# Attention on one core: the copy of the turned maxima and the scaling of x move from VectorE to ScalarE

## The chip, the cores and the metric

The kernel runs on one core of one Trainium2 chip. The metric is the device time of one execution in microseconds (us). The time before is the median of 3 runs. One further execution was taken with the profiler on; every row below comes from it.

## The reference, cut to what matters

The program computes two transformer blocks; the change touches only the first attention. There x has 16 sequences of 512 tokens with 128 channels:

```
x = x + attn(layernorm(x))          # layernorm: (x - mean) / sqrt(var + 1e-5), per token
q, k, v = split(layernorm(x) @ W_attn.T)    # 16 heads of 8 channels
scores  = q @ k.T / sqrt(8) + alibi bias, causal
y       = softmax(scores) @ v
```

The layernorm can be written in two ways that give the same numbers up to rounding: (x - mean) * rstd, or x * rstd + shift with shift = -mean * rstd.

## The kernel before, in words

`attention` handles the 16 sequences ("blocks" b = 0 to 15), each in 4 steps (st = 0 to 3) of 4 heads. Every engine runs its own hand-written list of steps (`steps`), and semaphores couple them. Three streams are skewed against each other:

- **Scores for the maximum.** TensorE makes 12 score units per step (S0 to S5, two units each, lines 364 and 368) into three PSUM buffers `psS`, used in turn. VectorE reduces each unit to its row maxima (`mx`, line 472). Unit n can start only when the reduction of unit n-3 is done.
- **Turning of the maxima.** After a step's 12 reductions VectorE splits the maxima into two bf16 parts (`mhl`, lines 481 and 483). In the next step TensorE turns them ("M", line 404) into the PSUM bank `psM`; an engine copies the 8x512 result to `mT` (line 464), and SyncE's queue places it as two rows of the query operand, where it is needed one step later.
- **Scores again, exponential, and values.** TensorE makes the scores once more, with the maximum subtracted (E0 to E5, line 383, three PSUM buffers `psE`), ScalarE takes the exponential of 12 units (line 532, k = 0 to 11), GpSimd clears the future entries (`clear_future`, line 281, one for each of four column groups j), and TensorE multiplies with the values (V0 to V3, line 395). V1 needs the exponentials 4 to 7 and the clearing j = 1 behind them. E5's two units need the exponentials 7 and 8.

TensorE's order in each step is written out in line 139: S0 E0 M V2 S1 E1 V3 S2 E2 S3 E3 V0 S4 E4 S5 E5 V1. V2 and V3 belong to the step before.

The input of a later block is prepared in between. In step 3 of block b VectorE computes mean and variance of block b+2 (`norm_stats`, lines 411 to 421), GpSimd raises the variance to the power -1/2 (`factors`, line 266), and VectorE writes the scaled x into `xn` (`norm_apply`, line 427) in front of its reduction 6. In step 0 of the next block TensorE turns `xn` (line 318) and projects it to q and k (line 324); ScalarE, VectorE (`split`, line 440) and GpSimd (lines 271 and 273) cut these into three bf16 parts, which go through memory into the operands. Blocks 0 and 1 are prepared before the steps begin. So there are 14 preparations inside the steps.

`psM` is one bank that is used in turn, eight times a block; `s_mr` counts its fillings and `s_mf` its releases.

Of the kernel before, what the change touches and what calls it, by code (L numbers as in the profile page):

```python
# [66 lines left out]
def attention(nc, x_all, ident, x_in, w_attnT, qkv_scr, y_scr, rec_scr, shared, c_ident, c_identb, c_maskq, c_rows, nb=NB):  # L67


    with ExitStack() as ctx:  # L70
# [15 lines left out]
        sync6 = sb("sync6", [P, 6], F32)  # L86
        mv = sb("mv", [P, TT, 2], F32)
        veps = sb("veps", [P, TT], F32)
        rstd = sb("rstd", [P, TT], F32)
        mhalf = sb("mhalf", [P, TT], F32)  # L90
        zeros = sb("zeros", [P, T], F32)
        warm = sb("warm", [P, 1], F32)
# [65 lines left out]
        def there(u):  # L158

            return not isinstance(u, int) or 0 <= u < G * nb  # L160
# [61 lines left out]
        def _(pool):  # L222
# [39 lines left out]

            def factors(b):
                pool.wait_ge(s_xn, b)
                pool.wait_ge(s_stat, 3 * b + 3)
                pool.tensor_tensor(rstd[:], veps[:], mhalf[:], ALU.pow).then_inc(s_rstd, 1)

            def split_rest(b, s):

# [139 lines left out]
        @block.vector  # L409
        def _(dve):  # L410
            def norm_stats(b):
                for t in range(TT):
                    bn = dve.bn_stats(stats[:, t], x_all[:, bass.ds(TT * b + t, 1), :].rearrange("p a c -> p (a c)"))
                bn.then_inc(s_stat, 1)
                dve.wait_ge(s_stat, 3 * b + 1)
                dve.tensor_copy(sync6[:], stats[:, TT - 1])
                for t in range(TT):
                    bn = dve.bn_aggr(mv[:, t], stats[:, t])
                bn.then_inc(s_stat, 1)
                dve.wait_ge(s_stat, 3 * b + 2)  # L420
                dve.tensor_scalar(veps[:], mv[:, :, 1], EPS, None, ALU.add).then_inc(s_stat, 1)

            def norm_apply(b, used):
                dve.wait_ge(s_rstd, b + 1)
                dve.wait_ge(s_mr, used)
                for t in range(TT):
                    i = dve.tensor_scalar(xn[:, t], x_all[:, bass.ds(TT * b + t, 1), :].rearrange("p a c -> p (a c)"),
                                          mv[:, t, 0:1], rstd[:, t:t + 1], ALU.subtract, ALU.mult)
                i.then_inc(s_xn, 1)

            dve.wait_ge(s_first, 80)
            norm_stats(0)
            norm_apply(0, 0)
            dve.memset(sync6[:], 0.0).then_inc(s_su, 1)
            dve.tensor_scalar(wT[:, 0], wT[:, 0], D ** -0.5, None, ALU.mult).then_inc(s_yc, 1)

            def split(b, s):
                dve.wait_ge(s_hi, 2 * b + s + 1)
                dve.wait_ge(s_lo, 2 * b + s)
                dve.tensor_tensor(rest[:], psM[:], parts[s][:, 0], ALU.subtract).then_inc(s_mf, 1)  # L440

            for s in range(2):
                split(0, s)
            norm_stats(1)
            norm_apply(1, 1)

            def step(n, b, st, last):
                g = st
                real = there(G * b)
                ahead = st == G - 1 and (not isinstance(b, int) or b + 2 < nb)  # L450
                if ahead:
                    dve.wait_ge(s_rest, REST)
                    norm_stats(b + 2)
                if st == 1 and not last:
                    split(b + 1, 1)
                if real and there(G * b + g - 1):
                    dve.wait_ge(s_hl, 2 * (G * b + g))
                for k in range(UN):
                    if k == 2:
                        if there(G * b + st - 1):  # L460
                            dve.wait_ge(s_mr, use_max(b, st, last) + 1)
                            if there(G * b + st - 2):
                                dve.wait_ge(s_mrow, 32 * (G * b + st - 1))
                            dve.tensor_copy(mT[:], psMb[0:2 * HG, 0:T]).then_inc(s_mf, 1)
                    if k == 6 and ahead:
                        norm_apply(b + 2, use_next(b, 0) + 1)
                    if real:
                        j, p, h0, nh = s_units[k]
                        u = UN * g + k
                        w = P * (j + 1)  # L470
                        dve.wait_ge(s_sr, UN * G * b + u + 1)
                        dve.tensor_reduce(mx[:, j, 2 * p + h0:2 * p + h0 + nh], psS[k % 3][:, 0:nh * w].rearrange("p (h k) -> p h k", h=nh),  # L472
                                          AX, ALU.max).then_inc(s_su, 1)
                    if k == 7 and st == 0 and not last:
                        split(b + 1, 0)
                if real:
                    dve.wait_ge(s_su, 1 + UN * G * b + UN * (g + 1))
                    if there(G * b + st - 1):
                        dve.wait_ge(s_mr, use_max(b, st, last) + 1)
                    by_half = mx[:].rearrange("p t (c h) -> p t c h", c=2)  # L480
                    dve.tensor_copy(mhl[:, :, :, 0], by_half).then_inc(s_hl, 1)
                    dve.wait_ge(s_hl, 2 * (G * b + g) + 1)
                    dve.tensor_tensor(mhl[:, :, :, 1], by_half, mhl[:, :, :, 0], ALU.subtract).then_inc(s_hl, 1)
            steps(dve, step, 1)
            dve.wait_ge(s_sum, 16)
            dve.reciprocal(sums[0][:], sums[0][:]).then_inc(s_inv, 1)

        @block.scalar
        def _(act):
# [9 lines left out]
            def copy_v(n, use):  # L499
                act.wait_ge(s_mr, use + 1)  # L500
                act.activation(vaug[n][:, :, :, 0:D], psM[:].rearrange("p (t h d) -> p t h d", t=TT, h=H), ACT.Copy)\
                   .then_inc(s_mf, 1)

            copy_x(0)
            for s in range(2):
                hi_part(0, s, s + 1)
            act.wait_ge(s_vinit, 3)
            copy_v(0, 3)
            act.activation(warm[:], ident[:, 0:1], ACT.Exp).then_inc(s_ex, 1)

            def copy_y(u, g):
# [5 lines left out]
            def step(n, b, st, last):  # L517
# [10 lines left out]
                for k in range(EN):  # L528
                    if there(u):
                        j, p, h0, nh = e_units[k]  # L530
                        act.wait_ge(s_er, EN * u + k + 1)
                        act.activation(probs[st % 2][j][:, 2 * p + h0:2 * p + h0 + nh, :].rearrange("p h q -> p (h q)"),  # L532
                                       psE[k % 3][:, 0:nh * W[j]], ACT.Exp).then_inc(s_ex, 1)
                        if k == 3 and there(u - 1):
                            copy_y(u - 1, st + 1)
                    if k == 5 and ahead:
                        hi_part(b + 1, 0, use_next(b, 1))
                    if k == 9 and ahead:
                        hi_part(b + 1, 1, use_next(b, 2))
                    if k == 7 and st == 2 and not last:  # L540
                        if isinstance(b, int) and b == 0:
                            act.wait_ge(s_vinit, 4)
                        copy_v(1 - n, use_next(b, 3))
# [1606 lines left out]
```

## Time and profile before

| | us |
|---|---|
| median of 3 runs | 1781.46 (1780.94 to 1782.33) |
| the profiled execution | 1782.71 |
| span of its instructions | 1781.0 |
| attention, from the start of the span to about | 745 |

Busy over the whole span, from the page: TensorE 1289.9 us (72%), VectorE 1214.9 us (68%), GpSimd 1030.5 us (58%), ScalarE 825.2 us (46%). In a row of the timeline stand the start in us, the time that the row covers, the engine, the line, the operation with its tiles, the number of instructions (x4), and in brackets how long the engine had been idle and what ended it. Starts that lie closer together than the durations mean that consecutive instructions overlap.

### The profile page before, as it was taken

To read this page: it belongs to the slowest core of one execution; us is meant where nothing else is said; L and a number is where in the kernel's file an instruction comes from. 1 tells how busy PE (TensorE), PEld (TensorE's weight loads), DVE (VectorE), ACT (ScalarE), POOL (GpSimd) and SP (SyncE) were. 2 spreads that over 40 slices of the span, in tenths; PEclk is the share of its full clock that TensorE was granted. 3 is DMA by queue.
4 is the path that set the end of the run, shared out by engine and by line. 5 is a ranking of instruction groups with operands and counts; after the bars stand their busy time and mean duration, and the time that the engine had idled before them with its cause. 6 is when DMAs were issued, how large, how long until landed. Compare 5 with 4: busy or idle time off the path is not lost. (4 is left out here: it accounts for less than half of the span.)

```text
span 1781.0 us, 34332 instructions
## 1 busy us (share of the span) xinstructions
PE 1289.9 (72%) x8762; PEld 705.7 (40%) x8763; DVE 1214.9 (68%) x3716; ACT 825.2 (46%) x2009; POOL 1030.5 (58%) x1071
## 2 busy tenths in 40 slices
PE   2888888888888888559116266626279999999996
PEld 1333333333333333158006233316246556555654
DVE  2777777777777778457662279877766666666663
ACT  0356666555555656501202166643334444444443
POOL 4455555554555554234005368968158888888886
PEclk9999999998999999855557665555579999999999
DMA  4433322322332333145004300300413333333332
GB/s 99 138 79 79 85 78 77 81 83 69 77 86 77 77 84 81 55 169 200 5 9 113 79 30 24 126 6 24 171 30 42 42 42 42 41 41 43 41 42 35
DMA packets 79454, 124.66 MB, mean 70 GB/s; under 512 B 22976, under 2 KB 47232, under 8 KB 75312
## 3 DMA queue, kind: packets, MB, share of 16 engines
q0 software_dynamic: 45568, 59.38, 18.4%
q1 hardware_dynamic: 25792, 51.63, 8.6%
q10 hardware_dynamic: 8032, 12.93, 2.0%
q8 instruction: 26, 0.43, 0.1%
q14 instruction: 36, 0.29, 0.1%
HBM read 65.65 MB, written 57.68 MB: 69 GB/s over the span
## 5 line engine op out<-in xcount | busy, mean ns | idle before, releaser
L472 DVE TENSOR_REDUCE mx<-psS 128x1 f32<-128x384 f32 (+3 forms) x768 | 426.2, 597 | 164.4 <-PE psS L368 155.0
L532 ACT ACTIVATE probs<-psE 128x512 f32<-128x512 f32 (+2 forms) x768 | 362.5, 529 | 236.7 <-PE psE L383 227.1
L281 POOL TENSOR_SCALAR_AFFINE_SELECT probs<-probs 128x512 f32<-128x512 f32 x256 | 162.3, 641 | 236.4 <-ACT probs L532 236.1
L1935 POOL DMA_INDIRECT out<-ex_y,ex_idx x144 | 236.5, 1643 | 47.9 <-issue 43.0
L395 PE MATMUL psY<-probs,vaug 128*32 128x512 f32 (+3 forms) x2048 | 209.3, 473 | 42.7 <-POOL probs L281 42.6
L364 PE MATMUL psS<-maskq,identb 128*128 128x128 bf16 (+1 forms) x768 | 161.6, 254 | 54.5 <-DVE mx L472 49.9
L1926 POOL DMA_INDIRECT ex_xg<-expert_tab,ex_idx x144 | 142.2, 988 | 66.0 <-issue 41.8
L364 PEld LDWEIGHTS psS<-maskq,identb 128*128 128x128 bf16 x768 | 64.0, 98 | 245.4 <-DVE mx L472 186.7
L1909 DVE SCALAR_TENSOR_TENSOR ex_h<-ex_psG,ex_w,ex_up 128x352 f32<-128x352 f32 x144 | 84.0, 584 | 111.3 <-ACT ex_w L2010 107.1
L383 PE MATMUL psE<-qop,kop 63*128 63x512 bf16 (+3 forms) x1024 | 141.7, 309 | 2.7 <-ACT probs L532 2.7
L368 PE MATMUL psS<-kop,qop 61*128 61x128 bf16 (+3 forms) x1024 | 142.3, 317 | 0.0
L1993 PE MATMUL ex_psY<-ah_w3s,ex_hT 128*128 (+1 forms) x864 | 133.3, 290 | 1.2 <-ACT ex_hT L2004 0.7
L2003 ACT ACTIVATE ex_hT<-ex_psH 128x256 f32<-128x256 f32 x144 | 55.4, 385 | 135.9 <-PE ex_psH L1969 135.9
L1993 PEld LDWEIGHTS ex_psY<-ah_w3s,ex_hT 128*128 128x128 f32 (+1 forms) x864 | 107.5, 191 | 21.9 <-issue 4.3
L1975 PE MATMUL ex_psU<-ah_w1s,ex_xT 128*128 x288 | 110.4, 465 | 0.5 <-ACT ex_xT L2014 0.5
L1976 PE MATMUL ex_psG<-ah_w2s,ex_xT 128*128 x288 | 109.9, 463 | 0.0
L2014 ACT ACTIVATE ex_xT<-ex_psX 128x128 f32<-128x128 f32 x144 | 40.0, 278 | 104.9 <-PE ex_psX L1962 104.7
L395 PEld LDWEIGHTS psY<-probs,vaug 128*32 128x32 f32 x2048 | 46.8, 112 | 88.1 <-POOL probs L281 46.7
L1962 PE MATMUL ex_psX<-ident,ex_xg 128*128 128x128 f32 x144 | 47.5, 330 | 39.1 <-DMA ex_xg<-expert_tab,ex_idx 38.5
L271 POOL TENSOR_TENSOR parts<-rest,zeros 128x512 bf16<-128x512 f32 x32 | 40.5, 1265 | 57.8 <-DVE rest L440 57.8
L1969 PE MATMUL ex_psH<-ident,ex_h 128*128 128x128 f32 (+1 forms) x432 | 72.2, 275 | 0.0
L2008 ACT ACTIVATE ex_up<-ex_psU 128x352 f32<-128x352 f32 x144 | 66.9, 464 | 8.0 <-PE ex_psU L1975 1.0
(314 smaller groups left out, 2558.7 us busy)
## 6 DMA issues: line engine op xcount, KB each, us to landing
y_scr<-ysb SPq DMA_DIRECT2D x64, 256.0 KB, 2.0
qkv_scr<-parts POOLq DMA_DIRECT2D x32, 384.0 KB, 3.0
qop<-qkv_scr POOLq DMA_DIRECT2D x32, 192.0 KB, 4.1
kop<-qkv_scr POOLq DMA_DIRECT2D x32, 192.0 KB, 4.9
expert_tab<-table_rows SPq DMA_DIRECT2D x1, 4352.0 KB, 14.4
qop<-qkv_scr POOLq DMA_DIRECT2D x32, 128.0 KB, 4.9
kop<-qkv_scr POOLq DMA_DIRECT2D x32, 128.0 KB, 6.3
pj_num<-y_scr SPq DMA_DIRECT2D x16, 256.0 KB
```

Of the source, the lines that this page charges most:

```text
L281: pool.affine_select(diag, diag, [[0, HG], [1, P]], ALU.is_ge, 0.0, base=0, channel_multiplier=-1).then_inc(s_msk, 1)
L364: pe.matmul(out[:, :, P * j:w], identb[:], maskq[:, 0:nh, :], start=True, stop=False, skip_group_check=True)
L368: mm = pe.matmul(out[:, h, :], half(qop[n], p, ROW_MAX)[:, hh, P * j:P * j + P], half(kop[n], p, ROW_MAX)[:, hh, 0:w], start=False, stop=( ...
L383: mm = pe.matmul(psE[u % 3][:, W[j] * h:W[j] * h + W[j]], half(kop[m], p, ROW_END)[:, hh, P * j:P * j + P], half(qop[m], p, ROW_END)[:, hh ...
L395: mm = pe.matmul(psY[32 * h:32 * h + 32, P * k:T], vaug[m_v][:, k, HG * e_v + h, :], probs[e_v % 2][k][:, h, :], start=(k == 0), stop=(k = ...
L472: dve.tensor_reduce(mx[:, j, 2 * p + h0:2 * p + h0 + nh], psS[k % 3][:, 0:nh * w].rearrange("p (h k) -> p h k", h=nh), AX, ALU.max).then_i ...
L532: act.activation(probs[st % 2][j][:, 2 * p + h0:2 * p + h0 + nh, :].rearrange("p h q -> p (h q)"), psE[k % 3][:, 0:nh * W[j]], ACT.Exp).th ...
L1926: pool.indirect_dma_start(xg[t % 4][:], None, ytab, bass.IndirectOffsetOnAxis(ap=idx[t % 8][:], axis=0))\
L1935: pool.indirect_dma_start(out, bass.IndirectOffsetOnAxis(ap=idx[t % 8][:], axis=0), y[m][:], None, compute_op=ALU.add).then_inc(s_sc[m], 16)
L1975: pe.matmul(psU[n][:, 0:DE], xT[n][:], flat(w1s[:, e, :]), start=True, stop=True).then_inc(s_g2, 1)
L1976: pe.matmul(psG[n][:, 0:DE], xT[n][:], flat(w2s[:, e, :]), start=True, stop=True).then_inc(s_g, 1)
L1993: i = pe.matmul(psY[:, 0:C], hT[m][0:wd, f], flat(w3s[0:wd, f, e, :]), start=(f == 0), stop=(f == len(FC) - 1))
```

## The change

Four things, all inside `attention`:

- The copy of the turned maxima (`psM` to `mT`) is done by ScalarE (`copy_max`), behind its exponential 1, instead of VectorE in front of its reduction 2. This is once a step, 64 times in all.
- The scaling of x is done by ScalarE (`normalise`) as x * rstd + shift, four instructions of 128x128 a block. In step 3 it stands between the exponentials 6 and 7. VectorE's `norm_apply` is gone.
- VectorE computes one thing more in `norm_stats`, the negated mean (128x4), and waits at its start until GpSimd has read the earlier one.
- GpSimd computes one thing more in `factors`, shift = minus * rstd (128x4), after a wait for its own power.

```diff
             def factors(b):
                 pool.wait_ge(s_xn, b)
-                pool.wait_ge(s_stat, 3 * b + 3)
+                pool.wait_ge(s_stat, 4 * b + 4)
                 pool.tensor_tensor(rstd[:], veps[:], mhalf[:], ALU.pow).then_inc(s_rstd, 1)
+                pool.wait_ge(s_rstd, 2 * b + 1)
+                pool.tensor_tensor(shift[:], minus[:], rstd[:], ALU.mult).then_inc(s_rstd, 1)
...
             def norm_stats(b):
+                if not isinstance(b, int) or b:
+                    dve.wait_ge(s_rstd, 2 * b)
...
                 dve.tensor_scalar(veps[:], mv[:, :, 1], EPS, None, ALU.add).then_inc(s_stat, 1)
+                dve.tensor_scalar(minus[:], mv[:, :, 0], -1.0, None, ALU.mult).then_inc(s_stat, 1)
-
-            def norm_apply(b, used):
-                dve.wait_ge(s_rstd, b + 1)
-                dve.wait_ge(s_mr, used)
-                for t in range(TT):
-                    i = dve.tensor_scalar(xn[:, t], x_all[:, bass.ds(TT * b + t, 1), :].rearrange("p a c -> p (a c)"),
-                                          mv[:, t, 0:1], rstd[:, t:t + 1], ALU.subtract, ALU.mult)
-                i.then_inc(s_xn, 1)
...
                 for k in range(UN):
-                    if k == 2:
-                        if there(G * b + st - 1):
-                            dve.wait_ge(s_mr, use_max(b, st, last) + 1)
-                            if there(G * b + st - 2):
-                                dve.wait_ge(s_mrow, 32 * (G * b + st - 1))
-                            dve.tensor_copy(mT[:], psMb[0:2 * HG, 0:T]).then_inc(s_mf, 1)
-                    if k == 6 and ahead:
-                        norm_apply(b + 2, use_next(b, 0) + 1)
...
+            def normalise(b, used):
+
+                act.wait_ge(s_rstd, 2 * b + 2)
+                act.wait_ge(s_mr, used)
+                for t in range(TT):
+                    i = act.activation(xn[:, t], x_all[:, bass.ds(TT * b + t, 1), :].rearrange("p a c -> p (a c)"), ACT.Identity,
+                                       bias=shift[:, t:t + 1], scale=rstd[:, t:t + 1])
+                i.then_inc(s_xn, 1)
+
+            def copy_max(b, st, last):
+
+                act.wait_ge(s_mr, use_max(b, st, last) + 1)
+                if there(G * b + st - 2):
+                    act.wait_ge(s_mrow, 32 * (G * b + st - 1))
+                act.activation(mT[:], psMb[0:2 * HG, 0:T], ACT.Copy).then_inc(s_mf, 1)
...
+                    if k == 1 and there(G * b + st - 1):
+                        copy_max(b, st, last)
+                    if k == 6 and st == G - 1 and (not isinstance(b, int) or b + 2 < nb):
+                        normalise(b + 2, use_next(b, 0) + 1)
```

Before the steps, `normalise(0, 0)` stands first on ScalarE and `normalise(1, 1)` behind its first `copy_v`.

**Step 3 of block 0 on VectorE**, from the first part of the statistics to the last reduction. In brackets stand the semaphores that an instruction waits for. Before:

```order
L413 BN_STATS stats<-x_all 128x6 [waits x_rest]
L413 BN_STATS stats<-x_all 128x6 x3
L416 COPY sync<-stats 128x6 [waits stat]
L418 BN_AGGR mv<-stats 128x2 x4
L421 TENSOR_SCALAR veps<-mv 128x4 [waits stat]
L472 TENSOR_REDUCE mx<-psS 128x2 [waits scores_ready,max_parts]
L472 TENSOR_REDUCE mx<-psS 128x2 [waits scores_ready]
L464 COPY mT<-psM 8x512 [waits max_rows,misc_ready]
L472 TENSOR_REDUCE mx<-psS 128x2 [waits scores_ready] x2
L472 TENSOR_REDUCE mx<-psS 128x1 [waits scores_ready] x2
L427 TENSOR_SCALAR xn<-x_all,mv,rstd 128x128 [waits misc_ready,rstd_ready]
L427 TENSOR_SCALAR xn<-x_all,mv,rstd 128x128 x3
```

Now:

```order
L419 BN_STATS stats<-x_all 128x6 [waits rstd_ready,x_rest]
L419 BN_STATS stats<-x_all 128x6 x3
L422 COPY sync<-stats 128x6 [waits stat]
L424 BN_AGGR mv<-stats 128x2 x4
L427 TENSOR_SCALAR veps<-mv 128x4 [waits stat]
L428 TENSOR_SCALAR minus_mean<-mv 128x4
L461 TENSOR_REDUCE mx<-psS 128x2 [waits scores_ready,max_parts]
L461 TENSOR_REDUCE mx<-psS 128x2 [waits scores_ready] x3
L461 TENSOR_REDUCE mx<-psS 128x1 [waits scores_ready] x8
```

The 12 reductions now stand behind each other; one small instruction more stands in front of the first.

**The same step on ScalarE.** Before:

```order
L532 ACTIVATE probs_0<-psE 128x512 [waits exp_in_ready] x4
L515 ACTIVATE ysb<-psY 128x512 [waits pv_done]
L532 ACTIVATE probs_1<-psE 128x384 [waits exp_in_ready] x4
L532 ACTIVATE probs_2<-psE 128x512 [waits exp_in_ready] x2
L532 ACTIVATE probs_3<-psE 128x256 [waits exp_in_ready] x2
```

Now:

```order
L539 ACTIVATE probs_0<-psE 128x512 [waits exp_in_ready] x2
L507 ACTIVATE mT<-psM 8x512 [waits max_rows,misc_ready]
L539 ACTIVATE probs_0<-psE 128x512 [waits exp_in_ready] x2
L522 ACTIVATE ysb<-psY 128x512 [waits pv_done]
L539 ACTIVATE probs_1<-psE 128x384 [waits exp_in_ready] x3
L498 ACTIVATE xn<-x_all,shift,rstd 128x128 [waits misc_ready,rstd_ready]
L498 ACTIVATE xn<-x_all,shift,rstd 128x128 x3
L539 ACTIVATE probs_1<-psE 128x384 [waits exp_in_ready]
L539 ACTIVATE probs_2<-psE 128x512 [waits exp_in_ready] x2
L539 ACTIVATE probs_3<-psE 128x256 [waits exp_in_ready] x2
```

The exponential 7, the last that V1 and its clearing need, now stands behind four instructions more.

## Rows read from the trace of the kernel before

**Rows 1.** Windows: attention; busy us (and count) of each engine, granted clock, DMA.

```profile
0.00:745.00 745.00, 599.20 (x5376) 229.32 (x5377) 543.80 (x1219) 423.00 (x899) 389.06 (x570) 0.95 0.32 83
```

**Rows 2.** Waits, 250 to 450 us: total us, times, longest.

```profile
PEld psS L364 <- DVE mx L472: 50.8, 112, 1.7
```

**Rows 3.** Timeline of a step without preparation: start, us, engine, line, [idle before].

```profile
684.86 0.40 DVE L464 COPY mT<-psM 8x512 bf16<-8x512 bf16 x1
...
685.71 3.45 DVE L472 TENSOR_REDUCE mx<-psS 128x2 f32<-128x512 f32 x6 [0.45 <-PE psS L368]
...
685.93 1.08 ACT L532 ACTIVATE probs<-psE 128x512 f32<-128x512 f32 x2 [0.69 <-PE psE L383]
...
688.20 1.07 PE L395 MATMUL psY<-probs,vaug 128*32 128x512 f32 x8
...
689.84 2.62 DVE L472 TENSOR_REDUCE mx<-psS 128x1 f32<-128x512 f32 x4 [0.68 <-PE psS L368]
```

**Rows 4.** Timeline of step 3 of a block, with preparation.

```profile
641.43 0.17 DVE L421 TENSOR_SCALAR veps<-mv 128x4 f32<-128x4 f32 x1
641.62 0.76 DVE L472 TENSOR_REDUCE mx<-psS 128x2 f32<-128x256 f32 x2
...
642.10 0.28 PE L364 MATMUL psS<-maskq,identb 128*128 128x256 bf16 x1 [0.85 <-DVE mx L472]
...
644.41 1.80 ACT L532 ACTIVATE probs<-psE 128x384 f32<-128x384 f32 x4
...
645.23 1.07 PE L395 MATMUL psY<-probs,vaug 128*32 128x512 f32 x8
...
646.27 0.64 POOL L281 TENSOR_SCALAR_AFFINE_SELECT probs<-probs 128x512 f32<-128x512 f32 x1 [1.52 <-ACT probs L532]
...
647.18 2.62 DVE L472 TENSOR_REDUCE mx<-psS 128x1 f32<-128x512 f32 x4 [0.18 <-PE psS L368]
...
647.40 1.89 ACT L532 ACTIVATE probs<-psE 128x512 f32<-128x512 f32 x4 [1.19 <-PE psE L383]
...
648.31 0.28 PE L383 MATMUL psE<-qop,kop 63*128 63x128 bf16 x4
648.52 0.85 PE L395 MATMUL psY<-probs,vaug 128*32 128x384 f32 x8
```

**Rows 5.** Timeline of ScalarE in the second attention, the same scaling there.

```profile
1064.53 1.66 ACT L1394 ACTIVATE mx_hn<-mx_ho,mx_nrm_shift,mx_nrm_rstd 128x128 f32<-128x128 f32 x4 [0.25 <-POOL mx_nrm_shift L1287]
1066.09 1.64 ACT L1364 ACTIVATE mx_xn<-x_all,mx_nrm_shift,mx_nrm_rstd 128x128 f32 x4
```

**Rows 6.** Timeline of VectorE in the second attention, two small instructions without a wait.

```profile
1068.95 0.16 DVE L1414 TENSOR_TENSOR mx_nrm_b<-mx_stats 128x8 f32<-128x8 f32 x1
1069.03 0.16 DVE L1415 TENSOR_TENSOR mx_nrm_minus_mean<-mx_stats 128x8 f32<-128x8 f32 x1
```

**Rows 7.** Groups by line and form, GpSimd: busy us, mean ns, idle before.

```profile
L1287 POOL TENSOR_TENSOR mx_nrm_shift<-mx_nrm_minus_mean,mx_nrm_rstd 128x8 f32<-128x8 f32 x13 | 2.7, 206 | 1.0
```

**Rows 8.** Timeline of the start of the program.

```profile
10.28 2.49 DVE L427 TENSOR_SCALAR xn<-x_all,mv,rstd 128x128 f32<-128x128 f32 x4 [1.26 <-POOL rstd L266]
...
12.91 1.09 PE L318 MATMUL psM<-ident,xn 128*128 128x128 f32 x4 [12.91 <-DVE xn L427]
```

**Rows 9.** Timeline of VectorE, four step marks.

```profile
209.27 2.31 DVE L472 TENSOR_REDUCE mx<-psS 128x2 f32<-128x512 f32 x4
...
218.68 2.30 DVE L472 TENSOR_REDUCE mx<-psS 128x2 f32<-128x512 f32 x4 [0.35 <-PE psS L368]
...
427.08 2.30 DVE L472 TENSOR_REDUCE mx<-psS 128x2 f32<-128x512 f32 x4
...
437.63 2.30 DVE L472 TENSOR_REDUCE mx<-psS 128x2 f32<-128x512 f32 x4 [0.57 <-PE psS L368]
```

**Rows 10.** Windows around the first and third mark; columns as in rows 1.

```profile
208.00:218.00 10.00, 8.44 (x84) 3.54 (x85) 9.14 (x23) 6.38 (x14) 3.58 (x5) 1.00 0.12 42
426.00:436.00 10.00, 8.79 (x71) 3.13 (x71) 8.31 (x20) 5.48 (x12) 3.58 (x5) 0.83 0.07 27
```

More of the change, by code:

```diff
@@ L88, in attention @@
         veps = sb("veps", [P, TT], F32)
+        minus = sb("minus_mean", [P, TT], F32)
         rstd = sb("rstd", [P, TT], F32)
+        shift = sb("shift", [P, TT], F32)
         mhalf = sb("mhalf", [P, TT], F32)
@@ L414, in norm_stats @@
                 bn.then_inc(s_stat, 1)
-                dve.wait_ge(s_stat, 3 * b + 1)
+                dve.wait_ge(s_stat, 4 * b + 1)
                 dve.tensor_copy(sync6[:], stats[:, TT - 1])
@@ L419, in norm_stats @@
                 bn.then_inc(s_stat, 1)
-                dve.wait_ge(s_stat, 3 * b + 2)
+                dve.wait_ge(s_stat, 4 * b + 2)
                 dve.tensor_scalar(veps[:], mv[:, :, 1], EPS, None, ALU.add).then_inc(s_stat, 1)
-            def norm_apply(b, used):
-                dve.wait_ge(s_rstd, b + 1)
-                dve.wait_ge(s_mr, used)
-                for t in range(TT):
-                    i = dve.tensor_scalar(xn[:, t], x_all[:, bass.ds(TT * b + t, 1), :].rearrange("p a c -> p (a c)"),
-                                          mv[:, t, 0:1], rstd[:, t:t + 1], ALU.subtract, ALU.mult)
-                i.then_inc(s_xn, 1)
+                dve.tensor_scalar(minus[:], mv[:, :, 0], -1.0, None, ALU.mult).then_inc(s_stat, 1)
             dve.wait_ge(s_first, 80)
             norm_stats(0)
-            norm_apply(0, 0)
             dve.memset(sync6[:], 0.0).then_inc(s_su, 1)
@@ L444, in _ @@
             norm_stats(1)
-            norm_apply(1, 1)
             def step(n, b, st, last):
@@ L483, in step @@
                     dve.tensor_tensor(mhl[:, :, :, 1], by_half, mhl[:, :, :, 0], ALU.subtract).then_inc(s_hl, 1)
-            steps(dve, step, 1)
+            steps(dve, step, 0)
             dve.wait_ge(s_sum, 16)
@@ L502, in copy_v @@
                    .then_inc(s_mf, 1)
+            def normalise(b, used):
[10 more added lines that the diff above has]
+                act.activation(mT[:], psMb[0:2 * HG, 0:T], ACT.Copy).then_inc(s_mf, 1)
+            normalise(0, 0)
             copy_x(0)
@@ L508, in _ @@
             copy_v(0, 3)
+            normalise(1, 1)
             act.activation(warm[:], ident[:, 0:1], ACT.Exp).then_inc(s_ex, 1)
```

## The prediction, made before the changed kernel was run

> **What bounds the kernel now.** I read the windows first. Attention takes 745 of the 1781.0 us; TensorE is busy for 599.20 us of it, VectorE for 543.80 and ScalarE for 423.00 [rows 1]. TensorE leads, but a busy share does not say what a microsecond on VectorE is worth. The waits say where the two touch: between 250 and 450 us the start of a score unit waited 112 times for a reduction, 50.8 us in all [rows 2]. So VectorE does hold TensorE up, and it is tempting to give every microsecond taken from VectorE to the time. The timeline shows whether the two moved pieces stand in those waits.
>
> The copy of the maxima does not. In a step without preparation it starts at 684.86 and takes 0.40, and then VectorE is idle for another 0.45 us until TensorE has made S1 [rows 3]. This step repeats to a few hundredths through the last blocks; steps 0, 1 and 2 of the other blocks also show idle time behind the copy.
>
> Step 3 is the tight one. The statistics delay the first reductions to 641.62, and TensorE waits 0.85 us for them [rows 4]. Later `norm_apply` stands in front of reduction 6. Its cost is read by comparing the same stretch with and without it. From the start of V0 to the start of reduction 8 it is 645.23 to 647.18, 1.95 us, in step 3, and 688.20 to 689.84, 1.64 us, in the plain step [rows 3, 4]. So 1.11 us of VectorE work costs TensorE 0.31 us.
>
> **The change, part by part.**
>
> *The copy leaves VectorE, 64 times.* VectorE only gets more idle time in front of reduction 2. I cost it at 0. The bounds are 0 and, for the 14 steps 3, where the statistics leave no idle time behind the copy, its whole 0.40: 14 x 0.40 = 5.6 us of gain. I take 0 because S1 itself comes late there (the 0.85 wait), so that reduction 2 waits for S1 and not for the copy.
>
> *The copy comes to ScalarE, 64 times.* Behind the exponential 1 ScalarE is idle for 0.69 us in the plain step [rows 3]. The copy reads 512 columns, as the exponential does; two of those take 1.08 us, so one takes about 0.6 and holds the queue for about 0.5. It fits, with 0.1 to 0.2 us to spare. Cost 0; if the cover is missed by 0.1 us each time, 64 x 0.1 = 6.4 us. The rows of maxima reach the operand a few tenths later and are needed a step later, so nobody waits.
>
> *`norm_apply` leaves VectorE, 14 times.* TensorE's S4 can come 0.31 us earlier.
>
> *The negated mean comes to VectorE, 14 times,* at the worst place, in front of the reductions for which TensorE already waits. Below, two small instructions without a wait start 0.08 us apart [rows 6]; above, the small instruction in front of the reductions takes 0.19 until the next start (641.43 to 641.62) [rows 4]. It has no wait of its own, so I take 0.10, near the lower end. The added wait at the head of `norm_stats` is met a block earlier: 0.
>
> *The product comes to GpSimd, 16 times.* 0.21 us and 0.08 in front of it (1.0 over 13) [rows 7]. In step 3 GpSimd then waits for exponentials anyway: 0. Before the steps it stands in front of the transfers of q and k, for which TensorE waits, so block 1's product costs 0.3 us.
>
> *The scaling comes to ScalarE, 14 times, between the exponentials 6 and 7.* The second attention has the same instruction, with shift and rstd as operands. Four of them follow four others after 1066.09 - 1064.53 = 1.56 us [rows 5]; that is what the queue is held for. Now the chain in step 3 [rows 4]. The exponentials 4 to 7 end at 644.41 + 1.80 = 646.21; with 1.56 of scaling and 0.10 for the negated mean, 647.87. The clearing followed 0.06 later and takes 0.64: 648.57. V1 can then start at about 648.63. Second path: exponential 8 starts 0.43 behind exponential 7, at 647.80, and ends at 648.40. E5's second unit needs it; its instruction and two more of 0.07 (0.28 for four) bring V1 to 648.46 + 0.21 = 648.67. V1 started at 648.52. So the 0.31 that `norm_apply` gives back never reaches V1; V1 comes 0.15 us later than before, on either path nearly the same. 14 x 0.15 = 2.1 us slower. S0, the turning of x and everything after stand behind V1 on TensorE, so this is kept.
>
> The Trainium skill has a rule against this move: ScalarE: Activation LUTs, section "Rules for kernel authors", says that multiplications and additions belong on VectorE. Going by it alone one would charge the difference of the engines' own times, 1.64 - 1.11 = 0.53 us, 14 times, 7.4 us; the sum here charges only what arrives at V1.
>
> *The start of the program.* The first scaling took 2.49 us on VectorE and x was turned at 12.91 [rows 8]. Now: 10.28 for the power's end, 0.08 for the negated mean, 0.29 for the product, 1.65 on ScalarE: 12.30 instead of 12.77. That is 0.4 us earlier, less the 0.3 above: 0.1 us gained. The Trainium skill (Advanced Engine Details and Errata, section "VectorE Performance Modes") says that GpSimd and two-port VectorE instructions block each other; the slow first scaling agrees, and by that rule alone the move would free 1.4 us here (2.49 - 1.11), of which the longer way through GpSimd and ScalarE takes back all but the 0.4.
>
> Sum of the chain: +2.1 - 0.1 = +2.0 us.
>
> *The granted clock.* This term is less certain. After TensorE's long wait in step 0 of each block the granted clock is for a short while at the lower of its two levels. Once, after GpSimd was late in one block, the work stood differently, and the clock fell in step 3 too. From one mark in step 3 to the mark in step 0 it took 437.63 - 427.08 = 10.55 us, against 218.68 - 209.27 = 9.41, with a clock of 0.83 in place of 1.00 [rows 9, 10]. So such a fall costs 1.1 us. What TensorE did before it was to wait, and the change makes the waits in step 3 longer (0.85 to 0.95, and the one at V1 is new), and it shifts every block by another 0.15 us. I expect about 3 such falls more: 3.3 us. The ends are 0 and one in every second block, 7 x 1.1 = 7.7. I take 3 because 12 of the blocks of the kernel before have only the one fall of step 0, while the blocks whose work had been displaced had a second.
>
> Total +5.3 us. The profiled execution would go from 1782.71 to 1788.0, its span from 1781.0 to 1786.3, and the median of the runs, which lies 1.25 below that execution, from 1781.46 to **1786.8**.
>
> **The rivals.**
>
> *A. V1 late, no more falls of the clock:* +2.0, 1783.5 us. For it: the 12 regular blocks are regular. Against it: the wait in step 3 that grows is the one next to which the clock had fallen.
>
> *B. The forecast:* 1786.8 us.
>
> *C. Faster.* VectorE's relief decides, and ScalarE's insert is hidden. The place is the stretch from V0 to V1 in step 3. It decides if ScalarE holds its queue for less than 1.56 - 0.15 - 0.21 = 1.2 us. Then S4 to V1 come 0.31 - 0.10 = 0.21 us earlier, 14 x 0.21 + 0.1 = 3.0 us: 1778.5; with part of the 5.6 us from the copy in step 3 it would be 1776. For it: VectorE is the engine that TensorE waits for. Against it: the four instructions cost 1.56 us in both rows.
>
> *D. The copy on ScalarE is not covered.* 0.1 us late in each of 64 steps, +6.4 + 2.0: 1789.9. For it: only 0.1 to 0.2 us to spare. Against it: consecutive instructions on ScalarE overlap.
>
> *E. The price of the rule above, in full:* 14 x (0.53 + 0.10) = 8.8: 1790.3. Against it: ScalarE was idle 1.19 us in front of the exponential 8 [rows 4].
>
> **How the numbers follow.** A 0.33, B 0.42, C 0.15, D 0.06, E 0.04. A measurement here can tell 0.2%, 3.6 us, from no change. Faster by more than that needs C with part of the copy, half of C and a little for what I overlook: 0.12. Slower by more: B, D, E, less the part of B with a single fall, plus the upper part of A: 0.50. Within: 0.38. As both signs are possible but slower leads, the range reaches from C, 1777.5, over A and B to seven falls, 1781.46 + 2.0 + 7.7 = 1791.2. B's own range is 1784.6 to 1791.2.
>
> **What would show it.** In step 3: the wait for the first reductions at 0.95; the stretch from V0 to reduction 8 back at 1.64; V1 waiting for GpSimd's clearing or E5 for an exponential. In the plain step: the same 8.7 us from step to step, idle time behind reduction 1 at about 0.9, and ScalarE's idle time there nearly gone. I am wrong if step 3 gets shorter, if the plain step changes, or if the granted clock of attention goes up from 0.95.

## The result, and the profile after

| | before | after |
|---|---|---|
| median of the runs | 1781.2 us (4 runs) | 1818.49 us (1813.63 to 1822.08, 4 runs) |
| ratio, with its 95% interval | | 1.0212 (1.0189 to 1.0235) |
| the profiled execution | 1782.71 | 1820.37 |
| span of its instructions | 1781.0 | 1818.6 |

The change costs 37.3 us. 5.3 were forecast, with 1791.2 us as the upper end of the range. (Some executions of most versions, the kernel before among them, are about 30 us longer; the ratios are meant to leave them out, medians can contain them, so versions are compared by their ratios below.)

The new time is a stall that the prediction does not contain. The waits of the changed kernel between 0 and 783 us (attention) have a row of a kind that the kernel before does not have for the reductions: an engine that waits for nothing the profile knows.

```profile
DVE mx L461 <- issue: 26.1, 5, 5.4
```

The timeline shows the first of the five, at the first reduction of step 0 of block 4.

```profile
220.53 0.76 DVE L461 TENSOR_REDUCE mx<-psS 128x2 f32<-128x256 f32 x2 [5.30 <-issue]
221.01 0.10 PEld L368 LDWEIGHTS psS<-maskq,identb 128*128 128x128 bf16 x1 [4.52 <-DVE mx L461]
```

The scores lie ready; VectorE does not reduce them for 5.30 us, and TensorE waits 4.52 us for a free buffer. Such waits make the row that answers to [rows 2], 250 to 450 us, longer and its longest 4.6 instead of 1.7 us:

```profile
PEld psS L368 <- DVE mx L461: 58.1, 101, 4.6
```

The other four gaps end at 314.04 (5.39), 407.53 (5.02), 506.82 (5.39) and 598.92 (5.02), with blocks 6, 8, 10 and 12: every second block, from the second turn on. Blocks 2 to 13 are a loop over pairs of blocks, turned six times, so it jumps back five times. What happens meanwhile is in the DMA view of 214 to 224 us: before, one queue alone carries packets there (the first line); after, a second one does (the second line):

```profile
q1 hardware_dynamic: 156, 0.27, 7.3%
```

```profile
q14 instruction: 3, 0.02, 0.7%
```

and in the page's third part, queues with packets and MB, before and after:

```profile
q14 instruction: 36, 0.29, 0.1%
```

```profile
q14 instruction: 61, 0.50, 0.1%
```

The queue that brings an engine its own instructions is silent at this place before; after, it carries packets of 8 KB there (0.50 MB in 61), and 25 more in all. That is five for each jump; three of them fall into this view, the others elsewhere in the turn. An instruction is 64 bytes long (the Trainium skill, Vector Engine (DVE) Microarchitecture Reference, section 1.2), so one packet holds 128 of them. No row contradicts this; none shows it directly, nor whose instructions a packet brings.

The rest of the change did nearly what was forecast. The windows of attention, as in [rows 1] (it is longer now, 0 to 783 us):

```profile
0.00:783.00 783.00, 612.61 (x5376) 229.35 (x5377) 508.54 (x1107) 474.29 (x1027) 390.38 (x586) 0.93 0.31 79
```

VectorE lost 35 us of work and ScalarE gained 51, and the granted clock went from 0.95 to 0.93. The timeline of step 3, against [rows 4]:

```profile
677.32 0.16 DVE L428 TENSOR_SCALAR minus_mean<-mv 128x4 f32<-128x4 f32 x1
677.42 0.88 DVE L461 TENSOR_REDUCE mx<-psS 128x2 f32<-128x256 f32 x2
...
677.90 0.28 PE L368 MATMUL psS<-maskq,identb 128*128 128x256 bf16 x1 [0.95 <-DVE mx L461]
...
678.75 0.20 POOL L270 TENSOR_TENSOR shift<-minus_mean,rstd 128x4 f32<-128x4 f32 x1
...
681.04 1.06 PE L399 MATMUL psY<-probs,vaug 128*32 128x512 f32 x8
681.52 1.64 ACT L498 ACTIVATE xn<-x_all,shift,rstd 128x128 f32 x4
...
682.68 2.62 DVE L461 TENSOR_REDUCE mx<-psS 128x1 f32<-128x512 f32 x4 [0.69 <-PE psS L372]
...
683.06 1.98 ACT L539 ACTIVATE probs<-psE 128x384 f32<-128x384 f32 x5
...
683.60 0.63 POOL L285 TENSOR_SCALAR_AFFINE_SELECT probs<-probs 128x512 f32<-128x512 f32 x1 [3.04 <-ACT probs L539]
...
684.29 0.85 PE L399 MATMUL psY<-probs,vaug 128*32 128x384 f32 x8
```

The wait for the first reductions is 0.95 us, as forecast. From V0 to reduction 8 it is 681.04 to 682.68, 1.64 us, as forecast. The scaling holds ScalarE's queue from 681.52 to 683.06, 1.54 us (1.56 forecast), exponential 7 and the clearing follow it, and V1 starts 0.06 us after the clearing.

A plain step, against [rows 3], with the copy now in ScalarE's idle time:

```profile
729.91 3.45 DVE L461 TENSOR_REDUCE mx<-psS 128x2 f32<-128x512 f32 x6 [0.77 <-PE psS L372]
...
730.13 1.08 ACT L539 ACTIVATE probs<-psE 128x512 f32<-128x512 f32 x2 [0.23 <-PE psE L387]
```

All later comparisons use the length of the steps: the distance between the starts of VectorE's casts of the maxima (`mhl`), from that of the step before to the step's own. Inside the loop steps 0, 2 and 3 repeat to 0.03 us in nearly all blocks, so a median over blocks 2 to 13 tells a few hundredths (blocks 2 and 8 apart, where GpSimd is late or the start still shows).

| us | step 0 | step 2 | step 3 |
|---|---|---|---|
| before | 9.93 | 9.80 | 10.15 |
| after | 10.20 to 10.29 (block 9: 9.93); at the jumps 16.35 to 17.40 | 9.88 | 10.02 |

Steps of the last block take 8.73 in both. The five steps 0 at the jumps sum to 83.3 us instead of 5 x 10.27 (their length in the shifted version below): **32.0 us of the 37.6** by which the profiled executions differ. 26.1 of it is VectorE's idle time, the rest stands in what is left of the same step, run at a lower clock (granted 0.73 between 220 and 230 us; 1.00 in this step before). Of the other 5.6 us, 3.5 stand up to the last cast of the maxima (762.91 against 727.43 us, less the 32.0) and belong to the attention; 2.1 stand behind it, in code that the change does not touch.

### The profile page after: what moved, and what is told of

Read it like the earlier page. It is cut to its first block and busy times, and to the rows that moved or that the text cites. A ratio compares the mean times of both kernels' runs of the same rounds, so it can differ in the third digit from the quotient of the medians.

```text
span 1818.6 us, 34402 instructions
## 1 busy us (share of the span) xinstructions
PE 1305.8 (72%) x8762; PEld 707.8 (39%) x8763; DVE 1179.3 (65%) x3604; ACT 875.7 (48%) x2137; POOL 1031.5 (57%) x1087
## 5 line engine op out<-in xcount | busy, mean ns | idle before, releaser
L387 PE MATMUL psE<-qop,kop 63*128 63x512 bf16 (+3 forms) x1024 | 148.5, 316 | 3.9 <-ACT probs L539 2.7
L387 PEld LDWEIGHTS psE<-qop,kop 63*128 63x128 bf16 x1024 | 58.4, 98 | 33.2 <-ACT probs L539 13.1
```

The costliest lines, as they stand in the source:

```text
L387: mm = pe.matmul(psE[u % 3][:, W[j] * h:W[j] * h + W[j]], half(kop[m], p, ROW_END)[:, hh, P * j:P * j + P], half(qop[m], p, ROW_END)[:, hh ...
```

## The experiments

The theory after the result: VectorE's instructions come in blocks of 128, and the loop is fetched again at the jump back when it touches four of these blocks instead of three. A program counts positions in VectorE's own list, register and branch instructions included: before, the loop stands at 184 to 488, after at 165 to 441 (a wait that stands by itself is counted with the instruction behind it). So the loop became shorter and the reload appeared; length alone cannot be the cause. The rival: something in the change's new waits.

**The change, its loop shifted.**

```diff
+            for k in range(20):
+                dve.memset(spare[:, k:k + 1], 0.0)
             dve.wait_ge(s_first, 80)
```

> The changed kernel with 20 tiny memsets on VectorE, put in front of its first wait where it is idle for 7 us; they only move VectorE's loop (276 instructions) from position 165 to 185, where the loop of the kernel before starts. Theory P (position: the 5.3 us that VectorE loses at the head of each of the 6 turns of its loop come from loading its own instructions again, because the loop now lies across one block of code more than before): no stall at the head, no burst of instruction loads there, ratio to the kernel before 1.000 to 1.004, and what is left is my sum of +2 us with or without a few falls of the clock. Rival W (the new wait or the negated mean, or the longer list of ScalarE, holds VectorE up there): the stall stays, ratio about 1.021.

Ratio 1.0057 (1.0019 to 1.0095), above the 1.000 to 1.004 expected. The interval is wide because two of the eleven times in it are 1807.23 and 1810.6 us; the mean of the other nine (1784.91 to 1792.37) gives 1.0043. No idle time at the jumps, 36 packets. 20 instructions that do nothing useful make the kernel some 28 us faster: the stall is one of position. The change without it is still slower than the kernel before. (The expectation counts six stalls; six turns have five jumps.)

**The kernel before, shifted by 90.**

```diff
+            for k in range(90):
+                dve.memset(spare[:, k:k + 1], 0.0)
             dve.wait_ge(s_first, 80)
```

> The kernel before with 90 tiny memsets on VectorE in front of its first wait: its loop (304 instructions) moves from position 184 to 274. If code is loaded in blocks of 128 instructions whose borders, as the two traces allow, lie at about 166 to 185 and every 128 further, the loop then lies across four blocks instead of three. Theory P: a stall of about 5 us at the head of each of the 6 turns, ratio about 1.020. Rival W: nothing changes, ratio 1.000.

Ratio 1.0145 (1.0081 to 1.021). Its timeline and its page:

```profile
217.88 0.76 DVE L475 TENSOR_REDUCE mx<-psS 128x2 f32<-128x256 f32 x2 [2.97 <-issue]
```

```profile
q14 instruction: 62, 0.51, 0.1%
```

Five gaps, 15.1 us in all. The kernel before can be given the stall without any part of the change. Its gaps are shorter than the 5 us expected; why is open. The gaps do not explain the whole ratio: 1.0145 is 25.8 us, while the profiled execution (1795.97 us, the shortest of the four) is 13.3 us above that of the kernel before; the other three took 1803.51 to 1814.72. The shift shows in one more place: in every second block the statistics take 1.12 us instead of 0.87, and step 3 is 10.39 instead of 10.14.

**Two more positions.** The kernel before with `range(128)` in the same edit, one whole block:

> The kernel before with 128 small clearings on VectorE at its start, in the time in which it waits for its first operand, so that its loop over pairs of blocks stands at instructions 312 to 616 of VectorE's list instead of 184 to 488. Nothing else is changed. Theory (VectorE's instructions are loaded in blocks of 128, and the loop is loaded again at each jump back when it touches four of these blocks instead of three): the shift is one whole block, so the loop touches three blocks as before: no idle time at the five jumps back, 36 packets on the instruction queue plus the few of the longer list, and a time within 0.3% of the kernel before. Rival 1 (the number of added instructions, or the length of the whole list, decides; the shift of 90 had cost 1.45%): at least 3 us of idle time at each of the five jumps and 1.4 to 2% slower. Rival 2 (the clearings themselves disturb the start): a few us slower with no idle time at the jumps.

Ratio 1.0008 (0.9992 to 1.0024), no gap, 37 packets: neither the number of clearings nor the length of the list counts. And the changed kernel with `range(84)`:

> The changed kernel with 84 small clearings on VectorE at its start: its loop stands at instructions 249 to 525 of VectorE's list instead of 165 to 441. Theory (blocks of 128 with a border between 166 and 184, so others between 294 and 312, 422 and 440, 550 and 568): the loop touches three blocks, as in the version shifted by 20, so no idle time at the five jumps back and 1.003 to 1.010 of the kernel before, as there. Rival (a shift of this size is bad by itself: the kernel before, shifted by 90 to 274 to 578, lost 3 us at each jump): five gaps of about 3 us and 1.02 of the kernel before.

Ratio 1.0038 (1.0019 to 1.0056), no gap, 36 packets. The positions together, with a border at 166 to 172 and every 128 behind (all other versions start at 185 or 188 and have no gap):

| version | loop | blocks touched | gaps | packets |
|---|---|---|---|---|
| before | 184 to 488 | 3 | none | 36 |
| before + 90 | 274 to 578 | 4 | 5 of 3.0 | 62 |
| before + 128 | 312 to 616 | 3 | none | 37 |
| after | 165 to 441 | 4 | 5 of 5.2 | 61 |
| after + 20 | 185 to 461 | 3 | none | 36 |
| after + 84 | 249 to 525 | 3 | none | 36 |
| last scaling-only version below | 172 to 462 | 3 | none | 36 |

The positions alone would also be met by blocks of some 118 to 137 instructions, or of about 64 with more of them allowed; that it is 128 rests on the size of the packets. What is shown is that the position decides; that the gap is the loading of instructions is argued from the packets.

**Only the scaling moved** (13 clearings keep the loop at 185). Against the changed kernel:

```diff
                 for k in range(UN):
+                    if k == 2:
+                        if there(G * b + st - 1):
...
+                            dve.tensor_copy(mT[:], psMb[0:2 * HG, 0:T]).then_inc(s_mf, 1)
...
-                    if k == 1 and there(G * b + st - 1):
-                        copy_max(b, st, last)
```

> Only the scaling of x moved to ScalarE (with the negated mean and the product on GpSimd); the copy of the maxima stays on VectorE; 13 memsets bring VectorE's loop to position 185. Theory P and my sum: no stall, +2 to +5 us, ratio 1.001 to 1.003, and V1 in step 3 waits for GpSimd's clearing or E5 for an exponential. Rival W: a stall of 5 us a turn here too, ratio 1.02. A third, that the relief of VectorE pays: ratio 0.998.

Ratio 0.998 (0.9947 to 1.0014), below the 1.001 to 1.003 expected, but it cannot tell a gain from none. Step 3 is 9.94, step 0 10.20: 0.21 us gained, 0.27 lost. V1 is late, by 0.06 us a block.

**Only the copy moved** (8 clearings, loop at 185). The same edit the other way round, against the kernel before:

```diff
-                    if k == 2:
...
-                            dve.tensor_copy(mT[:], psMb[0:2 * HG, 0:T]).then_inc(s_mf, 1)
...
+                    if k == 1 and there(G * b + st - 1):
+                        copy_max(b, st, last)
```

> Only the copy of the maxima moved to ScalarE; VectorE scales x as before; 8 memsets bring VectorE's loop to position 185. My sum: nothing, ratio 0.999 to 1.001. If the copy is not covered on ScalarE: up to 1.004, and the plain step is longer than 8.73 us. If VectorE's copy stood in the way in step 3: down to 0.997.

Ratio 1.0032 (1.0016 to 1.0049). Steps 2 and 3 of the loop are 9.88 and 10.23: the copy, costed at nothing, costs 0.08 us in each. Outside the loop (9.72 and 8.73) it costs nothing. That is 1.9 us of the 5.7 that the ratio stands for; the profiled execution has seven of the longest steps 1 where that of the kernel before has three (below). The timeline of VectorE at the end of step 2, before and then here, shows where:

```profile
288.93 2.62 DVE L472 TENSOR_REDUCE mx<-psS 128x1 f32<-128x512 f32 x4 [1.67 <-PE psS L368]
291.59 0.18 DVE L481 CAST mhl<-mx 128x16 bf16<-128x16 f32 x1
```

```profile
292.15 2.62 DVE L469 TENSOR_REDUCE mx<-psS 128x1 f32<-128x512 f32 x4 [1.67 <-PE psS L369]
294.90 0.17 DVE L478 CAST mhl<-mx 128x16 bf16<-128x16 f32 x1
```

From the reductions to the cast it takes 2.66 us before and 2.75 here. Nothing runs in between, but the instruction list of the loop differs there, before and here:

```
L477 REGISTER_ALU
L481 CAST mhl<-mx 128x8x2 [waits misc_ready,scores_used]

L474 REGISTER_ALU
L476 REGISTER_ALU [waits scores_used]
L478 CAST mhl<-mx 128x8x2 [waits misc_ready]
```

In the loop the value that a wait compares with is computed into a register. The cast waits for the turning of the maxima with the value that the copy has used already; with the copy gone, it must be computed here, and it stands behind the wait for the last reduction. So the two waits were swapped, the computation going ahead of that wait:

```diff
-                    dve.wait_ge(s_su, 1 + UN * G * b + UN * (g + 1))
                     if there(G * b + st - 1):
                         dve.wait_ge(s_mr, use_max(b, st, last) + 1)
+                    dve.wait_ge(s_su, 1 + UN * G * b + UN * (g + 1))
```

> Only the copy of the maxima is moved to ScalarE, as in the version before with the copy alone, and the two waits in front of VectorE's cast of the maxima change places: it waits for the turning of this step first and for its last reduction second. Theory (with the copy gone the register that holds the value of the first of these waits is no longer computed earlier for the copy; in the instruction list of the loop the computation now stands behind the wait for the last reduction, so it delays the cast by 0.09 us in the steps of the loop): with the waits swapped the computation is done before the last reduction ends; steps 2 and 3 inside the loop go back from 9.88 and 10.23 to 9.79 and 10.15 us, and the ratio to the kernel before from 1.0032 to 0.999 to 1.001. Rival (the copy itself delays something, through its transfer that is issued 0.3 us later or through ScalarE's queue): steps 2 and 3 stay at 9.88 and 10.23 us.

Steps 2 and 3 are 9.79 and 10.15, those of the kernel before; ratio 1.0013 (0.9984 to 1.0043), which alone would not have told. From the reductions to the cast:

```profile
329.68 2.62 DVE L469 TENSOR_REDUCE mx<-psS 128x1 f32<-128x512 f32 x4 [1.66 <-PE psS L369]
332.34 0.18 DVE L478 CAST mhl<-mx 128x16 bf16<-128x16 f32 x1
```

2.66 us again. Outside the loop the swap costs 0.07 us a step (8.80 instead of 8.73), so it is no free edit.

**The scaling where ScalarE is idle** (with the copy on VectorE). V1 was late because exponentials 7 and 8 stood behind all four instructions.

```diff
-                    if k == 6 and st == G - 1 and (not isinstance(b, int) or b + 2 < nb):
-                        normalise(b + 2, use_next(b, 0) + 1)
+                    if k in (7, 8) and st == G - 1 and (not isinstance(b, int) or b + 2 < nb):
+                        normalise(b + 2, use_next(b, 0) + 1, range(3) if k == 7 else range(3, TT))
```

> Only the scaling is moved to ScalarE (the copy of the maxima stays on VectorE; loop kept at position 185), and it stands where ScalarE is idle: three of its four instructions behind exponential 7, the fourth behind exponential 8, instead of all four between 6 and 7. Theory (V1 is late because exponentials 7 and 8 stand behind 1.56 us of scaling, and ScalarE is idle for 1.19 us in front of exponential 8): exponential 7 and the clearing of column group 1 come about 1.56 us earlier, the three instructions fill the idle time, V1 is not late; step 3 stays at 9.94 us and step 0 falls from 10.20 to 9.93 us. 14 x 0.21 = 2.9 us less than the kernel before, ratio 0.996 to 1.000. Rival (V1 is bound by something else, the reductions or the unit E5): step 0 stays at 10.20 us, and the ratio is that of the version with all four together, 0.998.

Ratio **0.9951** (0.9933 to 0.9969), 0.5%, and more than the 0.996 to 1.000 expected: the first version faster than both kernels. Its timeline of step 3:

```profile
338.62 1.80 ACT L550 ACTIVATE probs<-psE 128x384 f32<-128x384 f32 x4
...
339.44 1.07 PE L400 MATMUL psY<-probs,vaug 128*32 128x512 f32 x8
340.31 1.25 ACT L508 ACTIVATE xn<-x_all,shift,rstd 128x128 f32 x3
...
340.49 0.64 POOL L286 TENSOR_SCALAR_AFFINE_SELECT probs<-probs 128x512 f32<-128x512 f32 x1 [1.52 <-ACT probs L550]
...
342.43 0.85 PE L400 MATMUL psY<-probs,vaug 128*32 128x384 f32 x8
```

The clearing runs 1.05 us after V0's start instead of 2.56 in the whole change, and V1 follows V0 by 2.99 us instead of 3.25. Step 0 is back at 9.94, step 3 stays at 9.94. That is 2.9 us of the 7.7 by which the profiled executions differ (1774.97 against 1782.71). The rest is not in these steps: 2.3 us stand behind the last cast, in unchanged code, and step 1, 3.6 us shorter in sum, comes in three lengths, of which two blocks here had the shortest. Whether the change causes that is not shown. Windows over step 1 of blocks 11, 12 and 9, columns as in [rows 1]:

```profile
529.59:541.15 11.56, 9.14 (x96) 3.32 (x96) 8.35 (x16) 6.05 (x13) 8.26 (x11) 1.00 0.26 91
570.83:583.59 12.76, 10.43 (x96) 3.59 (x96) 8.44 (x16) 6.00 (x13) 8.24 (x11) 0.87 0.23 83
443.43:457.33 13.90, 11.56 (x96) 3.74 (x96) 8.44 (x17) 5.99 (x13) 8.24 (x11) 0.75 0.21 76
```

The same 96 matmuls at a mean granted clock of 1.00, 0.87 and 0.75: from one length to the next it is 1.2 and 1.1 us.

**The negated mean on GpSimd.** Step 3 still has the forecast 0.10 in front of its first reductions. Added to the version above, on GpSimd between power and product, and taken from VectorE:

```diff
+                pool.tensor_scalar(minus[:], mv[:, :, 0], -1.0, None, ALU.mult).then_inc(s_rstd, 1)
...
-                dve.tensor_scalar(minus[:], mv[:, :, 0], -1.0, None, ALU.mult).then_inc(s_stat, 1)
```

> As the version with the scaling in three and one, and the negated mean is computed by GpSimd between its power and its product instead of by VectorE in front of its first reductions. Theory (the negated mean costs its 0.10 us because TensorE waits for these reductions, and GpSimd is idle for 0.98 us before its next clearing): step 3 falls from 9.94 to 9.84 us, the wait for the first reductions from 0.95 to 0.85 us; 1.4 us less than the version beside it, ratio to the kernel before 0.995 to 1.000. Rival (GpSimd's extra work delays its clearing j = 0 or the scaling): step 3 does not get shorter.

Ratio 0.9952 (0.9934 to 0.997), step 3 still 9.94: the outcome of the rival, though nothing shows its cause, a late GpSimd. The negated mean costs nothing. Timelines of VectorE in front of the first reductions, first before, then here:

```profile
334.43 0.18 DVE L483 TENSOR_TENSOR mhl<-mx,mhl 128x16 bf16<-128x16 f32 x1
334.58 0.87 DVE L413 BATCH_NORM_STATS2 stats<-x_all 128x6 f32 x4
...
335.98 0.17 DVE L421 TENSOR_SCALAR veps<-mv 128x4 f32<-128x4 f32 x1
336.16 0.76 DVE L472 TENSOR_REDUCE mx<-psS 128x2 f32<-128x256 f32 x2
```

```profile
341.29 0.18 DVE L481 TENSOR_TENSOR mhl<-mx,mhl 128x16 bf16<-128x16 f32 x1
341.53 0.87 DVE L421 BATCH_NORM_STATS2 stats<-x_all 128x6 f32 x4
```

From `veps` to the reduction it is 0.18 us without the instruction, and 0.18 with it in the change (677.24 to 677.42). But the statistics start 0.24 us behind the maxima's second part instead of 0.15. There stands the wait that the change added at the head of `norm_stats`. It was left out of the version with three and one (the order holds without it):

```diff
             def norm_stats(b):
-                if not isinstance(b, int) or b:
-                    dve.wait_ge(s_rstd, 2 * b)
```

> As the version with the scaling in three and one (copy on VectorE), and the change's added wait at the head of the statistics is left out. It is not needed for the order: the scores of a block, for which VectorE has waited by then, come after the turning of that block's scaled x, which comes after the scaling and so after both of GpSimd's factors. Theory (the 0.10 us in front of the first reductions of step 3 come from computing the register of this wait, since the statistics start 0.24 us after the second part of the maxima instead of 0.15, while the negated mean costs nothing: 0.18 us from veps to the reduction with and without it): the statistics start 0.15 us behind, the wait for the first reductions is 0.85 us instead of 0.95, step 3 falls from 9.94 to 9.84 us, 1.3 us in all, and the ratio from 0.995 to 0.994. Rival (the negated mean costs the 0.10): step 3 stays at 9.94 us.

Step 3 is 9.86, ratio 0.9945 (0.9922 to 0.9968). The statistics start 0.15 us behind again, and the wait for the first reductions is 0.87:

```profile
349.79 0.18 DVE L479 TENSOR_TENSOR mhl<-mx,mhl 128x16 bf16<-128x16 f32 x1
349.94 0.87 DVE L418 BATCH_NORM_STATS2 stats<-x_all 128x6 f32 x4
...
351.42 0.16 DVE L427 TENSOR_SCALAR minus_mean<-mv 128x4 f32<-128x4 f32 x1
351.52 0.76 DVE L468 TENSOR_REDUCE mx<-psS 128x2 f32<-128x256 f32 x2
```

The steps show the 0.08; the ratio cannot tell it from 0.9951. This run takes away the wait together with the computing of its value. That a met wait as such is free, the steps outside the loop show: there the value is a constant, and step 3 of block 0 takes 9.74 us with the wait and without it.

**The same without the clearings.**

```diff
-            for k in range(16):
-                dve.memset(spare[:, k:k + 1], 0.0)
```

> The version beside it without the small clearings that shift VectorE's loop: the loop stands at instructions 172 to 462 instead of 188 to 478. Theory (a block border lies somewhere between 166 and 184): if it lies behind 172, the loop touches four blocks, with about 5 us of idle time at each of the five jumps back, 61 packets on the instruction queue, and a ratio near 1.014; if it lies at or ahead of 172, no idle time, 36 packets and the time of the version beside it. Both fit the theory, and the run halves the interval for the border. Rival (the clearings themselves, not the position, prevent the reload): idle time at the jumps wherever the border is; told apart only in the second case.

Ratio **0.9937** (0.9913 to 0.996), no gap on VectorE. The border lies at or ahead of 172, and the version with the lowest ratio (its interval overlaps the three before it) needs no filling: scaling on ScalarE in three and one, copy and statistics on VectorE, no added wait.

**The whole change mended**: the changed kernel with three of the diffs above, the 20 clearings, the scaling in three and one, and the swapped waits.

> The whole change with three things mended: VectorE's loop shifted by 20 small clearings to position 185, the scaling on ScalarE in three behind exponential 7 and one behind exponential 8, and the two waits in front of the cast swapped. Theory: each mend undoes its own loss, so steps 2, 3 and 0 inside the loop are 9.79, 9.94 and 9.93 us (9.88, 10.02 and 10.20 to 10.28 us in the shifted version without the other two), and the ratio to the kernel before is that of the version with the scaling in three and one, 0.995 (0.993 to 0.998): moving the copy gains nothing more. Rival 1 (VectorE's relief by the copy does shorten steps once nothing stands against it): ratio 0.993 or less, step 3 below 9.9 us. Rival 2 (the mends do not add): above 0.999.

Steps 0, 2 and 3 are 9.95, 9.79 and 9.95, within 0.02 of what was expected: each mend undoes its loss. The ratio, 0.9978, lies at the upper end of the theory (0.993 to 0.998), and its interval (0.9945 to 1.0012) reaches into rival 2, so it does not decide; steps outside the loop are 0.07 longer. By the steps, moving the copy gains nothing.

## Why the prediction was wrong, point by point

- **The sum left out a term.** It went through operations, waits and the clock, and took for granted that an engine has its instructions. The failed step is "VectorE only gets more idle time", costed at 0: what leaves VectorE also moves its loop in the list, from 184 to 165. Shown: 32.0 us, gone when the loop is shifted, and brought about in the kernel before by a shift.
- *The scaling:* V1 late by 0.15 us a block; measured 0.06. The mechanism was right (clearing j = 1 behind exponential 7); from V0 to V1 it is 3.25 us where the chain gave 3.34. Rival E, 0.63 us a block, falls.
- *`norm_apply`:* 0.31 us back in step 3; measured 1.95 to 1.64, right.
- *Negated mean and added wait:* "0.10" and "a block earlier: 0". Shown: 0 and 0.08 to 0.10. The wait is met at once, but its value has to be computed where VectorE is never idle. The sum was right by luck, the two terms being exchanged.
- *The copy off VectorE:* 0 forecast. Measured 0.08 in each of the steps 2 and 3 of the 12 blocks in the loop, 24 x 0.08 = 1.9 us. It was not the copy but the register that it had computed for another wait. Its bounds named only a gain. Besides, step 0 of every second block is 10.27 where the scaling alone gives 10.20; why is open.
- *The copy on ScalarE:* covered, as forecast. In the plain step ScalarE's idle time fell from 0.69 to 0.23, VectorE's behind reduction 1 rose to 0.77 (0.9 forecast), and the step stayed at 8.73. Rival D falls.
- *The start:* x was turned at 12.55 instead of 12.91, 0.36 earlier; 0.4 forecast.
- *The clock:* 1.1 us a fall, measured 1.1 to 1.2. But the three more falls were expected in step 3, and none came there: its steps 3 in the loop are 10.02 but for block 8, 11.47, which is long before too (11.29). What varies is step 1, and its number cannot be forecast to a few: step 1 was at its longest three times in the kernel before, four times after, six and seven times in the change shifted by 20 and with the copy alone.
- Without the reload the change is at 1.0038 and 1.0057 of the kernel before, 6.8 to 10.2 us. That is 1788.0 and 1791.4 us, one inside the range and one at its end, 1791.2. That it comes near the forecast of 5.3 us is in part luck, as 3.3 us of that were falls of the clock in step 3. Rival C (ScalarE's part hidden, V1 not late) became true once the scaling was put into the idle time.

## What to carry to other kernels

Before costing a move, count where each loop of each engine stands in that engine's list; a row "<-issue" of some us at the head of every turn, with packets on an instruction queue beside it, points to a reload, and a few idle instructions ahead of the loop removed it here. Inside a loop count a wait whose value is computed as an instruction, even one that is met: where the engine is never idle it cost 0.08 to 0.10 us, and so can a removed instruction whose wait shared its value. And place work moved to another engine by that engine's idle time: the same four instructions cost 0.06 us a block in one place and gave 0.21 in another.

## What the hardware showed unexpectedly

TensorE can stall in the same way, and not in every execution of one kernel. The profiled execution of the version with the negated mean on GpSimd took 1805.05 us, others of the same kernel, not profiled, 1772.31 to 1774.15. Its page and its waits:

```profile
q8 instruction: 71, 1.16, 0.3%
```

```profile
PE psM L324 <- issue: 21.9, 5, 4.5
```

Five stalls of 4.4 us on average at the same five jumps, on TensorE, and 71 packets on a second instruction queue that has 26 in the kernel before. Three other versions had such an execution profiled (the mended change and the two without the added wait); the lengths of their steps above leave out the steps 0 at the jumps. TensorE's list is the same in all versions, those without such stalls too, so position alone does not decide there. What does is open.
